# A mixture-of-experts layer: the second product laid out token by feature, its sum moved from PSUM to VectorE

## The reference

```python
xn = layernorm(x)
# relational graph convolution: 100000 edges, 16 relations
msg = (xn @ weight[rel])[src] * norm * sigmoid(gate[rel, src])
x = x + relu(segment_sum(msg, dst)) + linear_attention(xn)
# mixture of 8 experts, 2 chosen per token
t = layernorm(x)
probs = softmax(t @ router_w.T); rw, re = top_k(probs, 2); rw = rw / rw.sum()
combine = zeros(N, 8); combine[n, re] = rw
out = t
for e in range(8):
    h = gelu(t @ w1[e] + b1[e])
    out = out + combine[:, e:e+1] * (h @ w2[e] + b2[e])
x = x + out
```

## Time and profile before

| what | value |
|---|---|
| median of 3 runs | 1955.37 us (1952.18 to 1957.35) |
| the profiled execution | 1947.87 us, span 1946.0 us |
| PE busy | 1852.5 us, 95% |
| VectorE busy | 1152.4 us, 59% |
| ScalarE busy | 803.9 us, 41% |
| POOL busy | 769.8 us, 40% |
| mean granted clock of TensorE | 0.982 |

### The profile page before, as it was taken

The page is one execution under the profiler, slowest core; times in us unless marked ns, Lnnn a source line. Parts: engine busy times, 40 slices in busy tenths (PEclk is TensorE's granted clock), DMA queues, the critical chain, the costliest instruction groups (busy, mean ns, idle before and its releaser), DMA issues.

```text
span 1946.0 us, 28360 instructions
## 1 busy us (share of the span) xinstructions
PE 1852.5 (95%) x10189; PEld 1574.4 (81%) x10189; DVE 1152.4 (59%) x3290; ACT 803.9 (41%) x1454; POOL 769.8 (40%) x812
## 2 busy tenths in 40 slices
PE   5999999999997699998799999999999999999998
PEld 4878888888886599998688888888888887888987
DVE  6564555444443577777566767666676675766753
ACT  4555555555553333331133334333343343433443
POOL 2000000000000467667766666556566566556500
PEclk8999999999999799999899999999999999999999
DMA  7665777655552664444333343333434334233300
GB/s 215 227 230 212 282 292 286 227 224 222 214 203 118 250 233 142 155 132 154 106 112 104 105 125 93 114 98 109 122 88 124 102 101 133 67 117 108 96 17 16
DMA packets 113868, 295.55 MB, mean 152 GB/s; under 512 B 18106, under 2 KB 73778, under 8 KB 104406
## 3 DMA queue, kind: packets, MB, share of 16 engines
q1 hardware_dynamic: 75200, 189.27, 26.5%
q0 software_dynamic: 38528, 104.46, 18.5%
HBM read 162.70 MB, written 130.96 MB: 151 GB/s over the span
## 4 chain that ended last, share of the span: by engine, by line
PE 83%; DVE 6%; ACT 3%; DMA 3%; POOL 2%; issue 2%; SPq 1%; DVEq 0%; ACTq 0%
PE bank L51 21%; PE bank L53 19%; PE bank L52 19%; PE bank L1325 15%; POOL plain L582 2%; PE bank L1314 2%; PE bank L1424 2%; DMA messages<-plain 2%; DVE parts L612 1%; DVE plain L967 1%; PE bank L1371 1%; ACT parts L1148 1%; PE bank L1218 1%; DVE plain L801 1%; PE bank L1438 1%
## 5 line engine op out<-in xcount | busy, mean ns | idle before, releaser
L582 POOL DMA_INDIRECT plain<-messages,idxT x784 | 759.0, 968 | 1066.5 <-issue 873.4
L51 PE MATMUL bank<-parts 128*128 128x512 f32 (+1 forms) x1864 | 756.9, 406 | 29.4 <-DMA parts<-xnT_scratch 22.1
L53 PE MATMUL bank<-parts 128*128 128x512 f32 (+1 forms) x1864 | 722.1, 387 | 0.0
L52 PE MATMUL bank<-parts 128*128 128x512 f32 (+1 forms) x1864 | 719.9, 386 | 0.0
L51 PEld LDWEIGHTS bank<-parts 128*128 128x128 f32 x1864 | 353.3, 190 | 116.9 <-issue 34.5
L1325 PE MATMUL bank<-plain 128*128 128x128 f32 x3136 | 389.7, 279 | 24.3 <-DMA plain<-messages,idxT 18.9
L53 PEld LDWEIGHTS bank<-parts 128*128 128x128 f32 x1864 | 352.1, 189 | 70.6
L1325 PEld LDWEIGHTS bank<-plain 128*128 128x128 f32 x3136 | 378.1, 195 | 33.4 <-DMA plain<-messages,idxT 21.3
L52 PEld LDWEIGHTS bank<-parts 128*128 128x128 f32 x1864 | 353.9, 190 | 56.3
L1148 ACT CAST parts<-plain 128x512 fp32r<-128x512 f32 (+1 forms) x208 | 123.8, 595 | 396.9 <-DVE plain L967 396.9
L612 DVE TENSOR_TENSOR parts<-plain,parts 128x512 fp32r<-128x512 f32 (+2 forms) x242 | 161.9, 672 | 209.4 <-ACT parts L1148 143.2
(11 more groups left out here) (153 smaller groups left out, 1095.7 us busy)
## 6 DMA issues: line engine op xcount, KB each, us to landing
messages<-plain SPq DMA_DIRECT2D x48, 2048.0 KB, 6.8
parts<-xnT_scratch SPq DMA_DIRECT2D x20, 1024.0 KB, 5.3
xnT_scratch<-parts SPq DMA_DIRECT2D x98, 128.0 KB, 3.3
plain<-messages,idxT POOLq DMA_INDIRECT x784, 2.8
w_parts<-parts SPq DMA_DIRECT2D x32, 256.0 KB, 2.4
parts<-w_parts SPq DMA_DIRECT2D x4, 2048.0 KB, 20.1
plain<-in_x SPq DMA_DIRECT2D x48, 128.0 KB, 7.1
plain<-in_x SPq DMA_DIRECT2D x10, 512.0 KB, 4.3
```

Of the source, the lines that this page charges most:

```text
L51: e.matmul(out, left(0), right(0), start=start, stop=False)
L52: e.matmul(out, left(0), right(1), start=False, stop=False)
L53: return e.matmul(out, left(1), right(0), start=False, stop=stop)
L582: e.indirect_dma_start(msg[:, b % SLOTS, j, :], None, table_rows, bass.IndirectOffsetOnAxis(idxT[:, j, b:b + 1], 0)).then_inc(s_gather[b % ...
```

## The change

The second product is turned round. `h_p` is now the weights (128 tokens at a time) and `w2` streams (256 features), so that the result is token by feature: for each tile of 128 tokens six matmuls of 256 columns into half of bank 6 (tiles 0 and 1) or bank 7 (tiles 2 and 3). Each expert's result is complete in itself. A new step `y_add` lets VectorE multiply it with the token's combine weight (a scalar per partition, from `combB`) and add it to `acc`, one instruction per tile. The biases become a result of the same kind (`bias`, added without a weight). PE waits for the add of the same half one use earlier before it writes that half again (`free_y`). `spread`, the multiplication L967, `sum_out` and `sum_back` fall away, and the store follows the last add. `combB` gets a second buffer. `weigh` keeps only ScalarE's copy and VectorE's low part.

The order of a round: `y_add(g, x_)` stands behind the second `share` of its round, that is behind the `ready` step and the batch that follow `down(g, x_)`; `bias(g)` stands in the place of `sum_back`, before the first `share` of expert 0, and its add behind that `share`.

```diff
@@ the order
             if nxt[0] < GROUPS:
                 order.append(("up", *nxt))
-            if x_ == 0 and g:
-                order.append(("sum_back", g - 1, 0))
+            if x_ == 0:
+                order.append(("bias", g))
             if g + 1 < GROUPS and 0 <= step < READY:
                 ready(g + 1, step)
             share()
-            if x_ == 0 and g:
-                order.append(("sum_back", g - 1, 1))
+            if x_ == 0:
+                order.append(("y_add", g, X))
             if nxt[0] < GROUPS:
                 order.append(("weigh", *nxt))
             order.append(("down", g, x_))
             if g + 1 < GROUPS and 0 <= step + 1 < READY - 1:
                 ready(g + 1, step + 1)
             share()
+            order.append(("y_add", g, x_))
...
-        order.append(("sum_out", g, 0))
-    order += [("sum_back", GROUPS - 1, 0), ("sum_back", GROUPS - 1, 1)]
+        order.append(("store", g))
@@ VectorE
-            def weigh(g, x_):
+            def split_h(g, x_):
                 n, e_i = SIZE[g] * P, g * X + x_
-                e.wait_ge(s_spread, e_i + 1)
                 for f in range(KH):
-                    e.wait_ge(s_gelu, KH * e_i + f + 1)
-                    e.tensor_tensor(g_s[:, f, 0:n], g_s[:, f, 0:n], bank[2][:, 0:n], ALU.mult).then_inc(s_weight, 1)
                     e.wait_ge(s_h_high, KH * e_i + f + 1)
                     low(lambda i: h_p[:, e_i % 2, i, f, 0:n], g_s[:, f, 0:n]).then_inc(s_h_low, 1)
+
+            def y_add(g, x_):
+                s, K, u = g % 2, SIZE[g], y_use[g, x_]
+                for p in range(2):
+                    ks = range(2 * p, min(2 * p + 2, K))
+                    e.wait_ge(s_down, 2 * u + p + 1)
+                    if x_ == X:
+                        e.wait_ge(s_acc, turn_use["turn_norm", g, 1 if K > 2 else 0] + 1)
+                    else:
+                        e.wait_ge(s_y_add, 2 * u + p - 1)
+                    for k in ks:
+                        y = bank[6 + p][:, (k % 2) * D:(k % 2 + 1) * D]
+                        if x_ == X:
+                            m = e.tensor_tensor(acc[:, s, k, :], acc[:, s, k, :], y, ALU.add)
+                        else:
+                            m = e.scalar_tensor_tensor(acc[:, s, k, :], y, combB[:, s, 0, k, x_:x_ + 1], acc[:, s, k, :],
+                                                       ALU.mult, ALU.add)
+                    m.then_inc(s_y_add, 1)
@@ ScalarE
             def weigh(g, x_):
                 n, e_i = SIZE[g] * P, g * X + x_
                 if e_i >= 2:
-                    e.wait_ge(s_down, e_i - 1)
+                    before = divmod(e_i - 2, X)
+                    e.wait_ge(s_down, 2 * y_use[before] + 2)
                 for f in range(KH):
-                    e.wait_ge(s_weight, KH * e_i + f + 1)
+                    e.wait_ge(s_gelu, KH * e_i + f + 1)
                     e.copy(h_p[:, e_i % 2, 0, f, 0:n], g_s[:, f, 0:n]).then_inc(s_h_high, 1)
...
-                elif step == "sum_out":
-                    g, h = a
-                    n = SIZE[g] * P
-                    e.wait_ge(s_down, X * (g + 1))
-                    e.wait_ge(s_turn_back, xT_use["sum_out", g, h])
-                    e.copy(xT[:, 0:n], bank[6 + h][:, 0:n]).then_inc(s_xT_made, 1)
@@ TensorE
-            def spread(g, x_):
-                n, e_i = SIZE[g] * P, g * X + x_
-                if x_ == 0:
-                    e.wait_ge(s_misc, misc_use["turn_choice", g] + 1)
-                    e.wait_ge(s_pick, 1)
-                if e_i:
-                    e.wait_ge(s_weight, KH * e_i)
-                e.matmul(bank[2][:, 0:n], pick[0:2 * X, x_:x_ + 1].to_broadcast([2 * X, P]), combT[0:2 * X, 0:n],
-                         start=True, stop=True).then_inc(s_spread, 1)
+            def free_y(g, x_, p):
+                u = y_use[g, x_]
+                if u:
+                    e.wait_ge(s_y_add, 2 * u + p - 1)
+
+            def bias(g):
+                if g == 0:
+                    e.wait_ge(s_b2_low, 1)
+                e.wait_ge(s_misc, misc_use["turn_choice", g] + 1)
+                for p in range(2):
+                    free_y(g, X, p)
+                    for k in range(2 * p, min(2 * p + 2, SIZE[g])):
+                        for i in range(2):
+                            m = e.matmul(bank[6 + p][:, (k % 2) * D:(k % 2 + 1) * D], combT[0:2 * X, k * P:(k + 1) * P],
+                                         b2_p[0:2 * X, i, :], start=i == 0, stop=i == 1)
+                    m.then_inc(s_down, 1)
 
             def down(g, x_):
-                n, e_i = SIZE[g] * P, g * X + x_
+                e_i = g * X + x_
                 e.wait_ge(s_h_low, KH * (e_i + 1))
-                if e_i == 0:
-                    e.wait_ge(s_b2_low, 1)
-                if g and x_ == 0:
-                    e.wait_ge(s_xT_made, xT_use["sum_out", g - 1, 1] + 1)
-                for o in range(KH):
-                    y = bank[6 + o][:, 0:n]
-                    if x_ == 0:
-                        for i in range(2):
-                            e.matmul(y, b2_p[0:2 * X, i, o * P:(o + 1) * P], combT[0:2 * X, 0:n], start=i == 0, stop=False)
-                    for f in range(KH):
-                        m = three(e, y, lambda i: w2_p[:, i, f, x_, o * P:(o + 1) * P],
-                                  lambda i: h_p[:, e_i % 2, i, f, 0:n], False, x_ == X - 1 and f == KH - 1)
-                m.then_inc(s_down, 1)
+                for p in range(2):
+                    free_y(g, x_, p)
+                    for k in range(2 * p, min(2 * p + 2, SIZE[g])):
+                        for f in range(KH):
+                            m = three(e, bank[6 + p][:, (k % 2) * D:(k % 2 + 1) * D],
+                                      lambda i: h_p[:, e_i % 2, i, f, k * P:(k + 1) * P],
+                                      lambda i: w2_p[:, i, f, x_, :], f == 0, f == KH - 1)
+                    m.then_inc(s_down, 1)
```

More of the change, by code:

```diff
@@ L188, in gps_layer @@
             share()
+            order.append(("y_add", g, x_))
             if g + 1 < GROUPS and step + 1 == READY - 1:
                 ready(g + 1, READY - 1)
-        order.append(("sum_out", g, 0))
-    order += [("sum_back", GROUPS - 1, 0), ("sum_back", GROUPS - 1, 1)]
+        order.append(("store", g))
     assert len(closed) == BATCHES
-    misc_use, xT_use, turn_use, mix_use = {}, {}, {}, {}
-    order = [s for step in order for s in ([step, ("sum_out", step[1], 1)] if step[0] == "sum_back" and step[2] == 0 else [step])]
+    misc_use, xT_use, turn_use, mix_use, y_use = {}, {}, {}, {}, {}
     last_batch, mixes_done = {}, {}
@@ L201, in gps_layer @@
     for s in order:
[L202 removed]
+        if s[0] in ("mix", "mix_back", "turn_norm", "route", "turn_choice"):
             misc_use[s] = len(misc_use)
[L204 removed]
+        if s[0] == "y_add":
+            y_use[s[1:]] = len(y_use)
+        if s[0] == "mix":
             xT_use[s] = len(xT_use)
@@ L215, in gps_layer @@
     relus = [xT_use[s] + 1 for s in order if s[0] == "mix"]
-    backs = [s for s in order if s[0] in ("mix_back", "sum_back")]
+    backs = [s for s in order if s[0] == "mix_back"]
     acc_adds = {s: i + 1 for i, s in enumerate(backs)}
@@ L392, in gps_layer @@
             sem(n) for n in ("logits", "softmax", "exp", "top2", "comb_low", "turn_comb"))
-        s_up, s_gelu, s_spread, s_weight, s_h_high, s_h_low, s_down = (
-            sem(n) for n in ("up", "gelu", "spread", "weight", "h_high", "h_low", "down"))
+        s_up, s_gelu, s_h_high, s_h_low, s_down, s_y_add = (
+            sem(n) for n in ("up", "gelu", "h_high", "h_low", "down", "y_add"))
         def wait_table(e):
@@ L537, in sync_program @@
                     load_group_xnT(a[0] + 1)
-                elif step == "sum_back" and a[1] == KH - 1:
+                elif step == "store":
                     g = a[0]
                     s, full, n0 = g % 2, full_tiles(g), START[g] * P
-                    e.wait_ge(s_misc, misc_use["sum_back", g, 1] + 1)
-                    e.wait_ge(s_acc, turn_use["turn_norm", g, 1 if SIZE[g] > 2 else 0] + 1)
+                    e.wait_ge(s_y_add, 2 * y_use[g, X - 1] + 2)
                     if full:
@@ L1482, in tensor_program @@
                     up(*a)
-                elif step == "weigh":
-                    spread(*a)
+                elif step == "bias":
+                    bias(*a)
                 elif step == "down":
```

24 lines of the change are left out of this document (10 added, 14 removed).

## The result

The changed kernel takes 1930.29 us (median of four runs, 1928.54 to 1931.28), the kernel before beside it 1956.07 (1952.18 to 1957.35): a ratio of 0.9877, 95% interval 0.9862 to 0.9891. That is 24 us less (in medians 26), where the working gave 9. The time lies inside the range and on the forecast side; the size was missed by 15 us.

The account below looks back on a forecast made before the run. The expert stage was taken as bound by TensorE's dense matmul queue. Terms -78 + 13 + 1 + 33 + 17 + 5 = -9 us gave a profiled time of about 1939 and a median of 1946 us, range 1918 to 1978.

Parts of the forecast that it names:

- (1): Expert stage on PE: 104 spread matmuls, one per expert and group, go; at 0.58 us each, 60 us saved.
- (3): PE's waits on ScalarE's copies and VectorE's weighing, and a bias step that came late, go: 5.7 us saved.
- (2): The 26 sets of output transposes on PE go: 10.8 us saved.
- (4): Kernel end, last product to store: one add replaces copy, transposes and add; 1.8 us saved.
- Split and bias: Second product in 256-column matmuls, starts 0.120 us apart, costs PE 13.2 us; bias in one run of eight, +1 us.
- R2: Rival: 256-column matmuls start more slowly than 0.120 us; break-even 0.124, at 0.140 a median of 1993 us; chance 0.20.
- (a): After routing, PE waits for expert 5's add, queued on VectorE behind routing and a batch: 33 us lost.
- (b): The first product behind the bias waits for the bias add, in nine groups behind a batch add: 17 us lost.
- (c): Expert 2's add stands behind mix_back(1) and its statistics on VectorE, so PE waits: 5 us lost.
- R1: Rival: PE's waits on the adds are hidden anyway, up to 55 us fall away, median 1891 us; chance 0.17.
- R3: Rival: VectorE's lag reaches more places than counted, 0.3 us more per expert, 31 us, median 1977 us; chance 0.15.
- R4: Rival: gathers on GpSimd become the bound, a few us at most, median 1950 us; chance 0.05.

Follow-up runs that it names:

- the best version: The changed kernel with every add directly behind its second product and the product's halves going round three banks: 1869.61 us, 0.957 of the kernel before.

## Why the size was missed

The net of the removal and of what PE gets, without stalls, was forecast as -78 + 13 + 1 = -64 us. It is -78 between profiles of like clock and -84 in medians. The stalls were forecast at 55; with what follows them they cost 60 to 62. The mechanism was right, and these terms of the sum had the wrong size:

**(1) Spreads, right.** 60 us stood, 59 are measured between the profiles. That is partly luck: a spread ahead of a product costs a little more than 0.58, and the 13 at expert 0 cost much less.

**(3) Waits: a step that failed.** "Waits: ... 5.7", it said, with "some us on everything else together" left aside. By the view it rested on, the kernel before had 13.9 us of waits without the gathers and the best version (that of the last experiment) has 1.8: 12.1 us went. The 7.5 us in ten small waits were not counted. Those on the split and the batch add, 5 us, are gone in the run without spreads and weighing, as are the spreads' own; those of the output's transposes are gone in the best version only.

**(2), (4) Output and end.** 12.6 us forecast without waits, 10.5 measured (9 to 15), and the end shows its 2.4 us. Right.

**Split and bias: the other step that failed.** 0.120 per start is right, so R2, which needed 0.124, falls, and with it the fully exposed load, 0.226. By its formula for an isolated matmul the Trainium skill (TensorE: Matmul & The Clock Gate, section Back-to-back issue gap) would have an estimated 0.109 at 256 columns; the rows say 0.120, as the line through 512 and 384 did. The bias: in the changed kernel eight pieces take (1446.03 - 1445.71 - 0.23) + 1.13 = 1.22 us; in the kernel before one pair takes 0.74,

```profile
1215.76 0.39 PE L53 MATMUL bank<-parts 128*128 128x512 f32 x1
1216.08 0.73 PE L1438 MATMUL bank<-parts 16*128 16x512 f32 x2
1216.73 0.50 PE L51 MATMUL bank<-parts 128*128 128x512 f32 x1
```

(0.32 - 0.23 + 0.65), so two pairs 1.48: a gain of 0.26 x 13 = 3 us, where +1 stood. One run of eight has two changes of rows, two pairs have four. Split and bias are 8 us together, where 14 stood.

**What the sum has now.** Spreads 59, output and end 12.6, waits 12.1, less 8: 76, where the profiles show 78. The 2 us left have no name but the short stretch of lower clock told below; the intervals of the ratios (about 3 us each side) are wider.

**From the profile to the median: a step that failed too.** "So the profiled time would be about 1939 and the median 1946": this let the 7.5 us between profile and median of the kernel before stand in the changed one. They do not: its profile took 1930.07 us and its median is 1930.29, both at 0.976; in the best version they are 1869.76 and 1869.61. The 7.5 us go with the lower granted clock of the usual execution of the kernel before; what sets that clock was not tested. Between the profiles the change is worth 17.7 us, between the medians 26 and 22.

**(a), (b), (c) Stalls: right, and not their whole price.** Route and statistics 38 us forecast, bias 17. The view shows 34.7 and 13.7, but counts from modelled ends. Set start against start with the best version, which issues the same matmuls in the same order, the waits on L980 cost 38.5 us and those on L978 16.0: 54.5 where 55 stood. The places are those of the text, the long ones too: without the second batch PE waits some 4 us. One of them in the changed kernel:

```profile
1188.04 0.39 PE L53 MATMUL bank<-parts 128*128 128x512 f32 x1
1192.04 0.55 PE L51 MATMUL bank<-parts 128*128 128x256 f32 x1 [3.62 <-DVE plain L980]
1192.39 0.41 PE L52 MATMUL bank<-parts 128*128 128x256 f32 x1
1192.61 0.41 PE L53 MATMUL bank<-parts 128*128 128x256 f32 x1
1192.82 0.42 PE L51 MATMUL bank<-parts 128*128 128x256 f32 x1
```

These rows show the part of the price that the sum did not have. Behind the stall 256-column products start 0.21 to 0.22 us apart and not 0.12: the clock stands at its lower level. Two windows, the first of the changed kernel around this stall, the second of the best version's whole expert stage:

```profile
1186.00:1206.00 20.00, 16.39 (x100) 15.09 (x99) 13.34 (x53) 6.55 (x10) 8.71 (x10) 0.83 0.18 54
```

```profile
985.00:1860.00 875.00, 872.10 (x6330) 821.91 (x6329) 633.83 (x1987) 329.11 (x535) 530.11 (x534) 1.00 0.36 107
```

The clock was left at full because no row of the kernel before has such a stall in its expert stage; there it fell once, for a short stretch behind waits of 1.6 and 0.7 us (0.91 granted in 1870 to 1890). From 985 us to its last product the changed kernel spends 27 us at the lower level (1.2 GHz and not 2.4), in six stretches that begin during or within 1.3 us of a stall: all three of about 4 us and three of the eight of 1.8 to 2.4. The best version spends none. In the same comparison, start against start, the matmuls in these stretches, stalls apart, lose 10 us (7 in the second profile of the changed kernel). Stalls and clock are 64.8; 60.4 is left, since the best version has a wait of 1.5 us of its own and the changed kernel happens to reach 985 us some 2 us earlier. The link of stall and clock is read from rows; no run held the clock up with the stall kept.

**The rivals.** R1 (waits hidden) fell: 33 stalls, none of the kinds missing. R3 (lag in more places) fell: 20 waits on L980 where (a) and (c) named 18 places, not one at every expert, and an add costs 1.65 / 4 = 0.41 us in a run of four. R4 fell: gathers 17.9 us, before 18.9.

So the forecast -9 becomes, between profiles, -78 + 60 = -18: 6 us more from waits, 6 from split and bias, 2 without a name, less 5 that clock and stalls cost over the forecast 55. In medians it is -84 + 62 = -22 in one series and -26 in the other, since the usual execution of the kernel before has a lower clock than the one that the sum was read from. The errors on what was taken away and on the clock go opposite ways, so the total is off by less than its parts.

## What to carry to other kernels

Where a change takes work off a full engine, count every row of that engine's waits, small ones too: here they came to 7.5 us and nearly all went. Before a sum made on one profile is set against a median, compare the granted clocks of the two executions. An operand with few rows between full ones costs more for the change of rows than for its columns; pad it with zeros, or put all such matmuls in one run. When an add moves behind an engine's in-order queue, put it ahead of the long chain or give the product one more bank: here both together turned 22 us into 84.

## What the runs showed of the hardware

- Matmuls in this format start 0.228, 0.174 and 0.120 us apart at 512, 384 and 256 columns; a weight load of 0.106 stays hidden even at 256.
- Going from weights of 128 rows to 16 and back costs about 0.4 us on top of the matmul's own start; padded to 128 rows with zeros the same matmul does not pay it (1926.63 against 1954.60 us).
- A stall of 4 us in a dense stream of matmuls was followed by the lower clock, at once in the rows above: some of a stall's price comes after it, here 7 to 10 us behind 33 stalls of 54.5 us in all.
- The time of the kernel before follows the granted clock: 1948 to 1950 us at 0.982 or 0.983, 1956 to 1959 at 0.974 to 0.977.
- Single parts of a change had another worth beside a kernel before at 2060 us than beside one at 1955: the spreads 41 to 44 us against 73, their padding 9 to 12 against 28.
